# Attention heads: the inverse's first 2x2 blocks made on GpSimd from a mask, and the unit of the low residual set on its diagonal

## The reference

```python
def step(Sst, inp):
    q_t, k_t, v_t, g_t, beta_t = inp
    Sst = Sst * jnp.exp(g_t)[..., None, None]
    kv = jnp.einsum('bhk,bhkv->bhv', k_t, Sst)
    delta = (v_t - kv) * beta_t[..., None]
    Sst = Sst + k_t[..., None] * delta[:, :, None, :]
    o = jnp.einsum('bhk,bhkv->bhv', q_t, Sst)
    return (Sst, o)
```

## Time and profile before

| | before |
|---|---|
| median of 3 runs | 1304.82 us |
| the profiled execution: its time, its span | 1303.8 us, 1302.0 us |
| busy in the span: PE, DVE, ACT, POOL | 1200.0, 1131.6, 975.0, 663.9 us |
| one key head in the steady stage (389.30 to 453.20) | 63.90 us |
| busy in that head: PE, DVE, ACT, POOL | 63.78, 59.73, 52.55, 34.14 us |
| TensorE clock granted in that head | 1.00 of full |

### The profile page before, as it was taken

The page is one execution under the profiler, slowest core; times in us unless marked ns, Lnnn a source line. Parts: engine busy times, 40 slices in busy tenths (PEclk is TensorE's granted clock), DMA queues, the critical chain, the costliest instruction groups (busy, mean ns, idle before and its releaser), DMA issues.

```text
span 1302.0 us, 35596 instructions
## 1 busy us (share of the span) xinstructions
PE 1200.0 (92%) x13356; PEld 1008.6 (77%) x13356; DVE 1131.6 (87%) x2092; ACT 975.0 (75%) x2076; POOL 663.9 (51%) x566
## 2 busy tenths in 40 slices
...
DMA packets 123893, 75.10 MB, mean 58 GB/s; under 512 B 93272, under 2 KB 116324, under 8 KB 122192
## 3 DMA queue, kind: packets, MB, share of 16 engines
...
## 4 chain that ended last, share of the span: by engine, by line
PE 79%; DVE 11%; issue 3%; ACT 2%; POOL 2%; DMA 2%; SPq 0%; POOLq 0%; DVEq 0%; ACTq 0%
PE bank L559 12%; PE bank L714 6%; PE bank L701 5%; PE bank L760 5%; PE bank L731 4%; PE bank L749 4%; PE bank L740 4%; PE bank L649 3%; PE bank L641 3%; PE bank L657 3%; DVE con L1056 2%; PE bank L609 2%; PE bank L610 2%; PE bank L1657 2%; PE bank L1682 2%
## 5 line engine op out<-in xcount | busy, mean ns | idle before, releaser
L1056 DVE SCALAR_TENSOR_TENSOR con<-bank,taps,con 128x1022 f32<-128x1022 f32 (+2 forms) x192 | 245.3, 1278 | 21.3 <-ACT con L829 16.7
L1214 POOL TENSOR_TENSOR gl<-const_sb,gc 128x512 f16<-128x512 f32 x128 | 130.0, 1043 | 120.7 <-DVE gc L1066 75.7
L559 PE MATMUL bank<-x,qkv 128*128 128x512 f16 x768 | 184.6, 392 | 6.4 <-DVE con L1056 6.3
L559 PEld LDWEIGHTS bank<-x,qkv 128*128 128x128 f16 x768 | 73.4, 100 | 89.1 <-issue 8.8
L1249 POOL TENSOR_TENSOR oo<-oo 128x512 f16<-128x512 f32 x64 | 76.1, 1199 | 121.8 <-ACT oo L959 121.8
L1114 DVE TENSOR_TENSOR X<-X,bank 128x512 f16<-128x512 f16 x160 | 108.8, 680 | 17.0 <-PE bank L649 15.7
L898 ACT ACTIVATE Z<-bank 128x512 f16<-128x512 f32 x160 | 96.4, 604 | 23.7 <-PE bank L657 23.7
L1105 DVE TENSOR_TENSOR Y<-bank,ymask 128x512 f16<-128x512 f32 x160 | 109.2, 683 | 2.9 <-PE bank L641 2.3
L829 ACT ACTIVATE con<-bank,taps 128x512 f32<-128x512 f32 x128 | 85.4, 687 | 33.1 <-PE bank L559 32.9
L1241 POOL TENSOR_TENSOR kd<-k_tok,gc 128x512 f32<-128x512 f32 x48 | 50.1, 1046 | 111.5 <-PE bank L740 111.5
L760 PE MATMUL bank<-out,sqo 128*128 128x256 f16 x768 | 96.2, 276 | 9.3 <-DMA sqo<-oo 9.2
...
...
## 6 DMA issues: line engine op xcount, KB each, us to landing
...
```

The source lines that it names most:

```text
L559: last = mm(bank[:, b], qkv16[:, w, a, t * P:(t + 1) * P], x16[:, x, a, b * S:(b + 1) * S], start=(a == k == 0), stop=(a == HT - 1 and k = ...
L1056: stt(out=out, in0=bank[:, 0:B, 0:S - k], scalar=taps[:, par, t, TAPS - 1 - k:TAPS - k], in1=out, op0=ALU.mult, op1=ALU.add).then_inc(tap_ ...
L1214: last = tt(gl[:, g % 2, k].rearrange("p (m r) d -> p m r d", m=2), upper.unsqueeze(1).unsqueeze(1).broadcast_to([P, 2, R, P]), gc[:, par, ...
```

## The change

Two parts of the inverse are done without PE:

- **x0.** `Z0` starts from `aH` itself: POOL multiplies it by the constant mask `turned_pairs` (1 on the diagonal, -1 on the pair's other element), one instruction per group after `aH`. The PE transposes, their PSUM bank and the ACT copies go. The product `p` at level 0 waits for POOL's `z0_ready`.
- **one.** The unit is put into the low residual: a POOL `affine_select` writes 1.0 on the diagonal of `res1` after DVE has stored it, and `Z` has three products per matrix for four. PE's `Z` waits for POOL's `res_low`.

Per head that is 16 transposes and 16 matmuls off PE, 2 copies off ACT, and 8 instructions of 128x512 onto POOL. The tables are written anew: the POOL steps are placed, `once` 3 comes before `solve` 1 and `turn` (1, 0) before `solve` 2 on PE and ACT, and `("once", 3)` moves from bank 7 to 5 and `("turn", (1, 0))` from 2 to 6. DVE's order is as before; it gets two small instructions at the start for the mask. A few small tiles are merged to make room.

```diff
-    (0, "solve", 0), (1, "gl", 3), (1, "aH", 1), (1, "decay", 2),
+    (0, "solve", 0), (0, "one", 1), (0, "one", 2), (1, "gl", 3),
...
-        def turn_start(n, par, h):
-            is_free(pe, n, ("st", 2 * h), ("st", 2 * h + 1), taking=("x0", h))
-            out = half16(take(n, "x0", h))
-            for j in range(8):
-                last = turn(out[:, j], X0[:, 8 * h + j], ident16[:])
-            filled(last, "x0", h)
...
-            is_free(pe, n, ("y", lh), ("turn", (l - 1, h)) if l else ("x0", h), taking=("p", lh))
+            if l == 0:
+                pe.wait_ge(z0_ready, 4 * n + 2 * h + 2)
+                is_free(pe, n, ("y", lh), taking=("p", lh))
+            else:
+                is_free(pe, n, ("y", lh), ("turn", (l - 1, h)), taking=("p", lh))
...
-            is_free(pe, n, ("res", g), ("once", g), taking=("Z", g))
+            pe.wait_ge(res_low, 4 * n + g + 1)
+            is_free(pe, n, ("once", g), taking=("Z", g))
...
-                mm(out[:, at], res0[:, g, j], Z0[:, u], start=False, stop=False)
-                last = mm(out[:, at], ident16[:], Z0[:, u], start=False, stop=True)
+                last = mm(out[:, at], res0[:, g, j], Z0[:, u], start=False, stop=True)
...
-        def turn_start(n, par, h):
-            is_full(act, n, ("x0", h), ("Z", 2 * h, 1), ("Z", 2 * h + 1, 1))
-            freed(do(Z0[:, 8 * h:8 * h + 8], half16(at_bank("x0", h)), ACT.Copy), "x0", h)
...
+            nc.vector.tensor_copy(turned[:, :, 0], unit[:, :, 0])
+            tt(turned[:, :, 1], unit[:, :, 1], unit[:, :, 0], ALU.subtract)
...
+        def turned_start(n, par, g):
+            pool.wait_ge(aH_ready, 4 * n + g + 1)
+            is_full(pool, n, ("Z", g, 1))
+            tt(Z0[:, 4 * g:4 * g + 4], aH[:, 4 * g:4 * g + 4], turned_pairs[:].unsqueeze(1).broadcast_to([P, 4, P]),
+               ALU.mult).then_inc(z0_ready, 1)
...
+        def residual_one(n, par, g):
+            is_free(pool, n, ("res", g))
+            nc.gpsimd.affine_select(out=res1[:, g], in_=res1[:, g], pattern=[[0, 4], [1, P]], base=0,
+                                    channel_multiplier=-1, compare_op=ALU.not_equal, fill=1.0)\
+                .then_inc(res_low, 1)
```

More of the change, by code:

```diff
@@ L65 @@
[L65 to L80, removed]
@@ L81 @@
-    (1, "once", 2), (1, "kd", 1), (2, "silu", 0), (1, "aL", 3),
-    (0, "op", 2), (2, "decay", 1), (0, "op", 3),
[5 rows of a table added]
+    (0, "sum", 0), (0, "sum", 1), (2, "proj", 1), (1, "p", (2, 1)),
+    (1, "load", "out"), (1, "pT", 3), (1, "y", (4, 0)), (0, "solve", 3),
+    (1, "turn", (3, 0)), (2, "tap", 1), (2, "gl", 2), (0, "power", 0),
+    (2, "decay", 0), (1, "y", (3, 1)), (0, "pdl", 3), (1, "p", (4, 0)),
+    (0, "sum", 2), (0, "sum", 3), (0, "sqo", 2), (0, "oT", 2),
+    (2, "silu", 1), (0, "sqo", 3), (1, "turn", (2, 1)), (1, "norm", 0),
@@ L83 @@
+    (0, "high", 2), (1, "res", 0), (0, "high", 3), (0, "op", 0),
+    (2, "proj", 0), (1, "once", 0), (2, "tap", 0), (1, "res", 1),
+    (0, "op", 1), (0, "low", 2), (0, "low", 3), (1, "res", 2),
+    (1, "Z", 0), (1, "once", 2), (1, "one", 0), (1, "kd", 1),
+    (2, "silu", 0), (1, "aL", 3), (0, "op", 2), (2, "decay", 1),
+    (0, "op", 3),
 ]
@@ L180 @@
     (1, "load", "z"), (1, "once", 2), (0, "op", 2), (2, "silu", 0),
-    (2, "decay", 1), (0, "low", 3), (0, "oT", 3), (1, "kd", 1),
-    (0, "op", 3), (1, "pT", 3),
+    (2, "decay", 1), (0, "low", 3), (0, "oT", 3), (1, "one", 0),
+    (1, "kd", 1), (0, "op", 3), (1, "pT", 3),
 ]
 LAST = [
-    (15, "load", "qkv"), (14, "kk", 0), (14, "gl", 3), (14, "load", "out"),
-    (14, "aT", 0), (13, "Z", 2), (14, "kk", 1), (13, "split", "out"),
-    (13, "once", 1), (14, "aT", 1), (13, "res", 3), (13, "solve", 0),
[19 rows of a table removed]
@@ L246 @@
-    (15, "unit", 1), (14, "solve", 3), (14, "sum", 1), (15, "p", (2, 1)),
-    (15, "aL", 0), (15, "turn", (3, 0)), (15, "y", (4, 0)), (14, "sqo", 2),
-    (14, "sqo", 3), (14, "pdl", 3), (15, "aL", 1), (15, "turn", (2, 1)),
[4 rows of a table removed]
-    (14, "high", 1), (15, "norm", 0), (15, "y", (4, 1)), (15, "turn", (3, 1)),
-    (14, "weigh", 2), (15, "res", 0), (15, "res", 1), (15, "p", (4, 1)),
-    (15, "once", 0), (14, "high", 2), (15, "unit", 3), (14, "z", 3),
-    (15, "Z", 0), (14, "weigh", 3), (14, "high", 3), (14, "op", 0),
@@ L273 @@
-    (15, "low", 0), (15, "high", 3), (15, "low", 1), (15, "weigh", 3),
-    (15, "op", 0), (15, "low", 2), (15, "op", 1), (15, "op", 2),
-    (15, "op", 3), (15, "low", 3),
+    (15, "load", "qkv"), (14, "kk", 0), (13, "one", 1), (13, "one", 2),
+    (14, "gl", 3), (14, "load", "out"), (14, "aT", 0), (13, "Z", 2),
+    (14, "kk", 1), (13, "split", "out"), (13, "once", 1), (14, "aT", 1),
+    (13, "res", 3), (13, "solve", 0), (14, "kk", 2), (13, "split", "z"),
[12 rows of a table added]
+    (13, "ks", 2), (13, "sqo", 1), (14, "y", (0, 1)), (15, "split", "qkv"),
[10 rows of a table added]
@@ new lines @@
+    (15, "tap", 3), (15, "load", "z"), (15, "proj", 3), (13, "z", 2),
+    (13, "z", 3), (15, "kT", 1), (15, "oT", 0), (13, "weigh", 2),
+    (13, "high", 1), (15, "v", (0, 1)), (14, "p", (4, 1)), (13, "weigh", 3),
+    (13, "low", 0), (15, "kT", 0), (14, "turn", (4, 0)), (14, "res", 0),
+    (13, "op", 0), (15, "v", (0, 0)), (13, "low", 1), (13, "high", 2),
+    (14, "once", 0), (15, "tap", 0), (13, "low", 2), (15, "proj", 0),
+    (13, "high", 3), (15, "silu", 3), (13, "op", 1), (14, "res", 1),
@@ new lines @@
+    (14, "res", 2), (14, "turn", (4, 1)), (14, "Z", 0), (14, "one", 0),
+    (13, "low", 3), (14, "once", 2), (13, "op", 2), (15, "silu", 0),
+    (15, "decay", 1), (15, "kk", 0), (15, "kk", 1), (14, "Z", 2),
+    (13, "op", 3), (15, "aT", 0), (15, "aT", 1), (14, "solve", 0),
+    (14, "once", 1), (14, "res", 3), (15, "decay", 2), (15, "aH", 0),
[3 rows of a table added]
+    (14, "split", "out"), (15, "gl", 2), (14, "pdl", 0), (15, "aH", 2),
[3 rows of a table added]
+    (14, "one", 1), (14, "one", 2), (15, "gl", 3), (14, "sqo", 0),
[7 rows of a table added]
+    (14, "sum", 0), (14, "qs", 3), (15, "unit", 1), (14, "solve", 3),
```

118 lines of the change are left out of this document (68 added, 50 removed), and 180 rows, old and new, of tables (BANK, FIRST, LAST, ORDER).

## The result

Median of 12 runs 1311.14 us (1309.24 to 1313.86), against 1304.85 for 12 runs of the kernel before on the same chip: ratio 1.0052, interval 1.0043 to 1.0061. The change made the kernel slower by 6.3 us, 0.5%. The profiled execution took 1309.93 us for a span of 1308.1, 6.1 longer than before.

The account below looks back on a forecast made before the run. PE was taken as the bound, except DVE's queue ahead of `st` 0. Per head +0.49 and -0.75 gave -0.26, over 14 heads -3.6 us, ends 0 +/- 1: 1301 us against 1304.8, range 1286 to 1310.

Parts of the forecast that it names:

- In the 13 us ahead of 433 the bound is DVE's queue: Steady head, ahead of `st` 0: DVE's queue up to `res` 3 sets the time; PE has just kept pace.
- The collision of `gl` 3 and `aT` 0: Ahead of `st` 0: two `one` steps delay `gl` 3 on POOL, so DVE's `aT` 0 waits; +0.49 us per head.
- `one` in bf16: POOL's `affine_select` of 128x512 on the low residual: taken as 0.64 us, bounds half of that and 1.07.
- The mask product at 1.1: POOL, ahead of `unit` 2: each `x0` product taken as 1.1 us, bounds 0.64 and 1.59.
- Rival B: POOL's queue sets the pace between 435.6 and 440.8, mask product 1.59 us: +0.64 per head, 1314 us; chance 0.19.
- The chain `unit` 2, `aH` 2, `dl`, `su` 1: Behind `st` 0: mask products delay `unit` 2, then ACT's `aH` 2 and `dl`; `su` 1 at 440.67, not 440.37.
- -0.75 behind it: Behind `st` 0, where PE is the bound: 0.75 us per head won of the 1.12 removed from PE.
- the first half's 0.45: Transposes of the first `x0` half, between `st` 0 and `su` 1: 0.45 us off PE, 0.15 of it left.
- the second half: Transposes of the second `x0` half, later in the head: part of the loss won back as `turn` (1, 0) fills PE's wait.
- Head 0 ... and the end of head 15 ... I put at 0 +/- 1: Both ends: head 0's first `p` waits for POOL, its transposes are gone; DVE bounds head 15's end; 0 +/- 1 us.

Follow-up runs that it names:

- e4: Changed kernel with `gl` 3 moved between `one` 1 and `one` 2 on POOL: 1306.56 us, 1.0017 to the kernel before.
- e9: Changed kernel with `one` on POOL for group 3 alone, heads 0 to 14; other unit products back on PE: 1302.66 us, 0.9984 to the kernel before.
- e5: Changed kernel with the `affine_select` of `one` 2 done twice, same values: 1321.48 us, 1.0125 to the kernel before.
- e12: e10 with `unit` 2 between the two mask products on POOL: 1297.41 us, 0.9941 to the kernel before.
- e7: Changed kernel, FIRST and LAST reordered (mask products, `once` 3, `unit` 2, `one` 3), head 15's unit product on PE: 1307.74 us, 1.0020 to the kernel before.
- e10: e9 with `once` 3 right behind `Z` 1 in FIRST, head 0's x0 on PE and ACT, LAST's `unit` 2 between mask products: 1299.23 us, 0.9957.
- e3: Changed kernel with `once` 3 put back to bank 7 and behind `solve` 1: 1310.76 us, 1.0051 to the kernel before.
- e11: e10 with ones set for all four groups in heads 0 to 14, POOL order `one` 1, `gl` 3, `one` 2: 1302.69 us, 0.9981.

## Why the prediction was wrong

I said 1301 and a fall of 3.8; it was 1311.1 and a rise of 6.3, 1 us outside my range. The profiled execution was to take 1300.2 and took 1309.9, 9.7 more. By the prediction's own steps:

- **"In the 13 us ahead of 433 the bound is DVE's queue": right.** e2 against the changed kernel removes the `one` part, puts the unit products back on PE, and a head is 0.37 us shorter (63.58 for 63.95).
- **The collision of `gl` 3 and `aT` 0: right, and about the right size.** Said: `aT` 0 takes 1.2 and `st` 0 comes +0.49. Measured: 1.25 and +0.57. PE's wait was said to grow from 0.27 to 1.4, counted by the starts of matmuls; by that count it is 1.28 (the 1.12 of the rows is counted from the end of the last one). e4 takes the whole 0.57 away, and in e9 and e2 it is gone too. e5 is no test of it: there the delay went to `su` 1. The Trainium skill, SBUF — State Buffer, section "Who interferes with whom", has a DVE instruction with two SBUF inputs and a GpSimd one take turns on shared ports; the 1.25 and e4's 0.69 agree, and so do `kk` and `res`, which have a PSUM source and keep their 0.68 beside POOL. `one` in bf16 took 0.64, the value chosen.
- **The mask product at 1.1: right.** 1.15 alone, 1.69 beside `aT` 2. By the Trainium skill, GPSIMD Engine Reference, section 3.1, it was an estimate of 1.11. Rival B, which needed 1.23 or more, falls: the kernel is slower, but not by B's mechanism. (B's own sum has a slip: 1.0 later on a gain of 0.75 is a loss of 0.25, not 0.15, which makes 1315 for 1314.)
- **The chain `unit` 2, `aH` 2, `dl`, `su` 1: right.** e12 shows it, where `unit` 2 one place forward shortens the way to `su` 1 by 0.30, and e5 from the other side. **Its term, "-0.75 behind it", was mis-sized: it measured -0.50.** Of the first half's 0.45 only 0.04 is left (I had 0.15), of the rest (`Z` 3 and the second half) 0.46 of 0.67 (I had 0.60). With +0.57 a head comes to about zero for -0.26, and heads 1 to 15 give -1.0 for -3.6 (-0.1 of it in heads 1 to 13, the rest in the last two). That is 2.6 of the 9.7 us missed.
- **"Head 0 ... and the end of head 15 ... I put at 0 +/- 1": this step failed, and it is the larger part.** It measured +7.1, from -1.35 ahead of `st` 0 (scatter), +4.86 in head 0 and +3.60 at the end. I had seen that head 0's first `p` waits for POOL, and had set the transposes that go against it without working it out. Three things showed in its place. First, POOL's queue in head 0 (two `aL`, two mask products, then `unit` 2) is in nobody's shadow: `p` 0 comes 1.5 later and `st` 3 1.8, and in e7, with `p` 0 on time, `st` 3 still comes 2.0 later. That the whole 2.2 up to 100 us are its doing isn't shown: the lower clock lasts 13.7 us of that stretch for 6.8 before, and e10 and e12, which are on time at `st` 3, lose 1.8 and 2.6 behind it. Second, the bank of `once` 3 has another last reader in head 0 than in the steady head, and with the wait for it the clock goes down (2.65, of it half each; e3 and e7 take it away, e2 and e9 have the wait without the clock). Third, in the last head `one` and `unit` 2 lie on PE's path (1.5, which e7 gives back). The prediction had no term for the clock at all: it was 1.00 in the steady head that I had read.

**What stays open.** Of the 7.1 us the +2.1 behind 1081 us weren't tied to the change: there PE waits 8.09 and 1.95 us for `sqo` by transposing DMAs, for 6.44 and 1.04 before. They start 2.0 us behind a load of expert weights, for 3.3 before. e7, e10, e11 and e12 don't have the loss; e2, with no `one`, does (1.8). The -0.9 over heads 13 to 15 has no cause that I could name. In the stretch from 68 to 100 us e10 and e12, of the same tables there, lie up to 2.2 us apart. The clock goes with that (down at 80.8 to 87.7 us in e12, and only at 89.5 to 93.0 in e10), but what takes it down at another time in one run than in the other stays open.
